# Computing edge features before a scatter instead of after it, and summing them from three bf16 parts, in a graph kernel on one core

## The chip, the cores and the metric

The kernel is one program on one core of a Trainium2 chip. The metric is the device time of one execution in microseconds, as the median of several runs. Engines are called as in the profile: PE (TensorE matmuls), PEld (its weight loads), DVE (VectorE), ACT (ScalarE), POOL (GpSimd), SP (SyncE).

## The reference, cut to what matters

A node table x (6250 x 256) goes through an adapter, a mixture of experts, two graph attention layers and a last mixture with its own attention. Only the adapter's edge part is touched here. 106,250 edges carry 32 numbers each:

```
time_feat = relu(edge_attr @ W_time.T + b_time)        # 106250 x 64
sums      = segment_sum(time_feat, src, num_segments=6250)
counts    = segment_sum(ones, src, num_segments=6250)
node_time_feat = sums / maximum(counts, 1)
```

`edge_attr` is edge_attr_32, the source node of an edge is `src`. The result joins the node features in the adapter's fusion product. Everything is float32.

## The kernel before, in words

`program` runs the stages in order, each a block in which every engine has its own instruction list: `setup`, `sorts` (to about 1413 us of the span), `edge_sums` (to about 2310 us), `norm_T`, `adapter`, normalisation, router and experts, two attention layers, a last attention and the last experts. Each stage ends when all its engines are done.

**sorts** (L218 to L430). Three lists of edges are brought into an order by node block (49 blocks of 128 nodes) and by slots in groups of 512 (256 groups for the list of this case, 4 columns of 128 edges each). DVE does it: it counts each block's edges (L380), PE adds the counts over the partitions (L331, L332), DVE reads these sums (L389) and makes the position of each edge with a match (L356), a scan (L357) and a predicated copy (L365) for each block. Positions of the first 208 of 832 columns (EARLY) are ready first (L401). DVE also makes the low seven bits of each edge's node, `lo0`, and for lists 1 and 2 a payload of 16 bytes for each edge (L420 to L428).

Meanwhile the 832 columns of the first list are moved: SP loads chunks of 16 columns (AC) of edge_attr_32 into a ring of four buffers (L294), ACT adds the low bits as a 33rd number (L322) and POOL scatters one column at a time with an indirect DMA (L274), 128 rows of 33 numbers (132 bytes) to `attr_sorted` in DRAM, which SP has filled with zeros and a node number that matches nothing (L304). A chunk's buffer is free when its scatters have landed (semaphores `done`): ACT and SP wait for that. PE has the sums and the turning of group ends (L335) of three sorts and nothing else.

**edge_sums** (L477 to L616). For each of 256 groups: ACT's queue loads 128 x 4 rows (L531, eight buffers ahead), DVE copies the 32 numbers together (L566), PE transposes them (L593), ACT copies the transpose out of PSUM (L516), PE multiplies it with a block matrix of four W_time (L611), DVE adds the bias (L559), ACT applies ReLU (L527). DVE makes four 128x128 matches of the low bits with 0 to 127 (L569), PE multiplies each with 64 features and a column of ones (L601, four products into pU), and DVE adds the 65 columns into the block's row of `acc` (L553); `grp[0]` says which block a group belongs to. All is float32, for which a product counts as two matmul instructions and two weight loads; a transpose counts as one. The engines run one to four groups apart (`ring`, L621).

At the same time POOL runs `scatter_pool` (L437 to L453): the first 384 columns of list 1, each an indirect DMA of 128 rows of 16 bytes (L449), in two sets of 16 with a wait for the set before. Later stages scatter the rest of lists 1 and 2 in the same way: `norm_T` columns 384 to 440, `adapter` 440 to 588, and so on. The adapter's DVE work has whole-tile additions of 128x1024 (L1357, L1363).

Of the kernel before, what the change touches and what calls it, by code (L numbers as in the profile page):

```python
# [83 lines left out]
class Kernel:  # L84
# [54 lines left out]
    def setup(self, keep):  # L139
# [22 lines left out]
        self.attr_sorted = nc.dram_tensor("attr_sorted", (NG0 * GE, ED + 1), F32).ap()  # L162
# [55 lines left out]
    def sorts(self):  # L218
# [4 lines left out]
        with ctx:  # L223
# [11 lines left out]
            rows = sb("rows", [P, AR, AC, ED + 1])  # L235
            st, dl, var = sb("st", [P, NB, 6]), sb("dl", [P, NB]), sb("var", [P, NB])
            pre = ps("pre", [P, 2, NB])
            zpay = sb("zpay", [P, FILL, PW], I32)
            zattr, zrow = sb("zattr", [P, 8 * (ED + 1)]), sb("zrow", [1, D + 3])
            s_zpay, s_zattr = sem("s_zpay"), sem("s_zattr")  # L240
# [6 lines left out]
            NC = ET // AC  # L247
# [3 lines left out]
            def _(pool):  # L251
                z3 = zattr[:, :].rearrange("p (r c) -> p r c", c=ED + 1)
                pool.memset(z3[:, :, 0:ED], 0.0).then_inc(s_zattr, 1)
                pool.memset(z3[:, :, ED:ED + 1], float(P)).then_inc(s_zattr, 1)
# [9 lines left out]
                for c in range(NC):  # L264
                    j = c % AR
                    pool.wait_ge(ld[j], 16 * (c // AR + 1) + (16 if c == NC - 1 else 0))
# [5 lines left out]
                    for k in range(AC):  # L272
                        t = c * AC + k
                        pool.indirect_dma_start(  # L274
                            out=self.attr_sorted, out_offset=bass.IndirectOffsetOnAxis(ap=pos0[:, t:t + 1], axis=0),
                            in_=rows[:, j, k, :], in_offset=None,
                            bounds_check=last, oob_is_err=False).then_inc(done[j], 16)
# [4 lines left out]
            def _(sp):  # L282
# [6 lines left out]
                def chunk(c):  # L289
                    j = c % AR  # L290
                    if c >= AR:
                        sp.wait_ge(done[j], 16 * AC * (c // AR))
                    n = min(AC, EM - c * AC)
                    sp.dma_start(rows[:, j, 0:n, 0:ED],  # L294
                                 i["edge_attr_32"][0:P * EM, :].rearrange("(p t) a -> p t a", p=P)[:, c * AC:c * AC + n, :])\
                        .then_inc(ld[j], 16)
                    if n < AC:
                        sp.dma_start(rows[0:EL, j, n, 0:ED], i["edge_attr_32"][P * EM:E0, :]).then_inc(ld[j], 16)
# [18 lines left out]
            def _(act):  # L317
                act.wait_ge(s_lo0, 1)
                for c in range(NC):
                    if c >= AR:  # L320
                        act.wait_ge(done[c % AR], 16 * AC * (c // AR))
                    nc.scalar.activation(rows[:, c % AR, :, ED], lo0[:, c * AC:(c + 1) * AC], ACT.Copy).then_inc(s_lo, 1)  # L322
# [4 lines left out]
            def _(pe):  # L327
                for n in range(3):
# [3 lines left out]
                    nc.tensor.matmul(pre[:, 1, :], self.ones[:, :], tot[:, :], start=True, stop=True).then_inc(s_pre, 1)  # L332
                    pe.wait_ge(s_gs, n + 1)
# [3 lines left out]
                    ins.then_inc(s_gt, 1)  # L337

# [138 lines left out]
    def edge_sums(self, acc, scatter=()):  # L477

        nc, i = self.nc, self.i
        ctx, sb, ps, sem = self.scope()  # L480
        A1 = AD + 1
        with ctx:
            rows = sb("rows", [P, DRING, K, ED + 1])
            attr = sb("attr", [P, DRING, K * ED])
            attrT = sb("attrT", [P, 2, P])
            tf = sb("tf", [P, 2, K, A1])
            S = sb("S", [P, DRING, K, P])
            wt = sb("wt", [P, K * AD])
            bt = sb("bt", [P, K, AD])
            pre = sb("pre", [P, 2, K * AD])  # L490
            pT, pF, pU = ([ps(f"{x}{n}", [P, 512]) for n in range(2)] for x in ("pT", "pF", "pU"))
            ld = [sem(f"s_ld{j}") for j in range(DRING)]
            s_w, s_z, s_at, s_T, s_Tc, s_F, s_tf, s_S, s_U, s_acc, s_pre = (sem(x) for x in (
# [1803 lines left out]
```

## Time and profile before

| | us |
|---|---|
| median of 3 runs | 10431.0 (10423.12 to 10436.96) |
| span of the profiled execution | 10342.3 |
| around the span, to the median | 88.7 |
| sorts, in the span | 0 to 1413 |
| edge sums, in the span | 1413 to 2310 |

The profile is one execution. "x" before a number is a count of instructions, busy time is given in us and the mean of one instruction in ns. "remote" stands for a wait that ended by a semaphore whose sender's record had ended before; "issue" is time in which an engine waited for nothing that the profile shows. PEclk is the granted clock of TensorE as a share of full speed: 1.00 is 2.4 GHz, 0.50 is 1.2 GHz.

### The profile page before, as it was taken

To read this page: it belongs to the slowest core of one execution; us is meant where nothing else is said; L and a number is where in the kernel's file an instruction comes from. 1 tells how busy PE (TensorE), PEld (TensorE's weight loads), DVE (VectorE), ACT (ScalarE), POOL (GpSimd) and SP (SyncE) were. 2 spreads that over 40 slices of the span, in tenths; PEclk is the share of its full clock that TensorE was granted. 3 is DMA by queue.
4 is the path that set the end of the run, shared out by engine and by line. 5 is a ranking of instruction groups with operands and counts; after the bars stand their busy time and mean duration, and the time that the engine had idled before them with its cause. 6 is when DMAs were issued, how large, how long until landed. Compare 5 with 4: busy or idle time off the path is not lost. (4 is left out here: it accounts for less than half of the span.)

```text
span 10342.3 us, 116779 instructions
## 1 busy us (share of the span) xinstructions
PE 5494.0 (53%) x22610; PEld 3209.3 (31%) x22610; DVE 5413.1 (52%) x18917; ACT 3566.1 (34%) x11436; POOL 5780.8 (56%) x5781
## 2 busy tenths in 40 slices
PE   0000001593221149936777764777771388888897
PEld 0000000481110025523444432444441134434445
DVE  8577400492200012226666654666663287788777
ACT  0000000241000012214666642666661176666662
POOL 3787767307567740044666654666666566566650
PEclk9999975795565569967878876888885577677658
DMA  4111100010000000002333321333330111111113
GB/s 128 24 21 22 23 11 4 22 40 3 2 23 1 1 1 0 0 12 84 91 91 91 92 64 57 92 91 91 92 89 2 25 23 22 23 23 24 22 22 101
DMA packets 476242, 426.24 MB, mean 41 GB/s; under 512 B 269726, under 2 KB 409876, under 8 KB 475668
## 3 DMA queue, kind: packets, MB, share of 16 engines
q0 software_dynamic: 214016, 282.62, 11.8%
q1 hardware_dynamic: 224020, 120.13, 4.3%
q10 hardware_dynamic: 37632, 17.48, 0.7%
q8 instruction: 159, 2.61, 0.1%
q14 instruction: 415, 3.40, 0.1%
HBM read 341.50 MB, written 78.72 MB: 41 GB/s over the span
## 5 line engine op out<-in xcount | busy, mean ns | idle before, releaser
L449 POOL DMA_INDIRECT pay_sorted<-pay,pos x1856 | 1883.4, 1015 | 1893.7 <-PEq L1217 721.2
L790 POOL DMA_INDIRECT G<-tab_gat,pay x1856 | 1770.4, 954 | 1187.3 <-issue 465.5
L790 POOL DMA_INDIRECT G<-tab_rt,pay x1216 | 1151.5, 947 | 816.0 <-PE pLU L867 353.0
L864 PE MATMUL pU<-G,PM 128*128 128x257 f32 x3712 | 1269.6, 475 | 324.3 <-ACT PM L961 191.4
L274 POOL DMA_INDIRECT attr_sorted<-rows,pos x832 | 972.9, 1169 | 411.3 <-issue 253.4
L864 PEld LDWEIGHTS pU<-G,PM 128*128 128x128 f32 x3712 | 808.2, 241 | 485.4 <-ACT PM L961 235.6
L1679 DVE TENSOR_TENSOR t<-pO,BL 128x1024 f32<-128x1024 f32 (+1 forms) x78 | 90.7, 1163 | 1345.3 <-remote 871.0
L1078 DVE TENSOR_REDUCE mt<-pW 128x4 f32<-128x2048 f32 x304 | 695.4, 2287 | 163.5 <-issue 77.6
L810 PE MATMUL pA<-identb,G 128*20 128x128 bf16 (+1 forms) x3072 | 438.6, 250 | 477.8 <-issue 202.8
L1663 ACT ACTIVATE H<-pH,B 128x512 f32<-128x512 f32 (+1 forms) x312 | 206.6, 663 | 1364.6 <-remote 691.2
L909 ACT ACTIVATE aT<-pA 20x256 bf16<-20x256 bf16 (+1 forms) x1232 | 512.3, 416 | 457.1 <-PE pA L810 170.5
L1626 PE MATMUL pO<-WL,H 128*128 128x256 f32 x1176 | 288.8, 401 | 573.6 <-issue 345.7
L1167 DVE SCALAR_TENSOR_TENSOR e<-e 128x256 f32<-128x256 f32 x928 | 396.2, 427 | 366.8 <-ACT e L955 292.8
L955 ACT ACTIVATE e<-pW,adst 128x256 f32<-128x256 f32 x928 | 438.0, 472 | 298.8 <-DVE mt L1051 209.4
L961 ACT ACTIVATE PM<-pP 128x256 f32<-128x256 f32 x928 | 339.6, 366 | 574.0 <-PE pP L836 380.6
L810 PEld LDWEIGHTS pA<-identb,G 128*20 128x20 bf16 (+1 forms) x3072 | 190.2, 98 | 1081.4 <-issue 1064.6
L836 PE MATMUL pP<-ident,PT 128*128 128x128 f32 x1856 | 490.6, 354 | 0.0
L1051 DVE TENSOR_REDUCE mt<-pW 128x1 f32<-128x256 f32 x928 | 389.6, 420 | 189.5 <-PE pW L820 136.9
L1175 DVE SCALAR_TENSOR_TENSOR acc<-acc,alpha,pU 128x257 f32 x928 | 442.5, 477 | 77.8 <-PE pU L864 41.2
L970 ACT ACTIVATE PT<-e,bias 128x256 f32<-128x256 f32 x928 | 458.3, 494 | 0.7 <-DVE e L1167 0.7
L322 ACT ACTIVATE rows<-lo 128x16 f32<-128x16 f32 x52 | 11.6, 229 | 1291.8 <-DMA attr_sorted<-rows,pos 1223.4
L593 PE MATMUL pT<-ident,attr 128*128 128x128 f32 x256 | 76.0, 297 | 708.5 <-issue 674.4
(324 smaller groups left out, 12213.3 us busy)
## 6 DMA issues: line engine op xcount, KB each, us to landing
pay_sorted<-pay,pos POOLq DMA_INDIRECT x1856
G<-tab_gat,pay POOLq DMA_INDIRECT x1856
G<-tab_rt,pay POOLq DMA_INDIRECT x1216
expert_parts<-pos SPq DMA_DIRECT2D x144, 128.0 KB
yl<-expert_parts SPq DMA_DIRECT2D x36, 512.0 KB, 4.0
attr_sorted<-zattr SPq DMA_DIRECT2D x1, 16896.0 KB, 53.2
rows<-attr_sorted ACTq DMA_DIRECT2D x256, 66.0 KB
attr_sorted<-rows,pos POOLq DMA_INDIRECT x832
```

Source lines behind the costliest of these rows:

```text
L274: pool.indirect_dma_start(out=self.attr_sorted, out_offset=bass.IndirectOffsetOnAxis(ap=pos0[:, t:t + 1], axis=0), in_=rows[:, j, k, :], i ...
L449: pool.indirect_dma_start(out=out, out_offset=bass.IndirectOffsetOnAxis(ap=self.pos[g][:, lo + n:lo + n + 1], axis=0), in_=self.pay[g][:, ...
L790: pool.indirect_dma_start(out=G[:, j, k, 0:R], out_offset=None, in_=table, in_offset=bass.IndirectOffsetOnAxis(ap=pay[:, g % (2 * PART), k ...
L810: ins = nc.tensor.transpose(pA[j % len(pA)][:, k * P:(k + 1) * P], parts[:, k, 0:ROWS], self.identb[:, :])
L836: ins = nc.tensor.transpose(pP[j % 2][:, k * P:(k + 1) * P], PT[:, j % 2, k * P:(k + 1) * P], self.ident[:, :])
L864: ins = nc.tensor.matmul(u[:, 0:F], PM[:, j % 2, k * P:(k + 1) * P], G[:, j, k, 0:F], start=(k == 0), stop=(k == K - 1))
L909: a.activation(aT[:, j % 2, :], pA[j % len(pA)][:, 0:K * P], ACT.Copy).then_inc(s_aT, 1)
L955: a.activation(e[:, j % 2, :], pW[j % 2][:, 0:K * P], ACT.Identity, bias=ad).then_inc(s_y, 1)
L970: a.activation(PT[:, s, :], e[:, s, :], ACT.Exp, bias=bias[:, j % 4:j % 4 + 1]).then_inc(s_PT, 1)
L1078: v.tensor_reduce(mt, pW[:, :, :], AX.X, ALU.max).then_inc(s_max, 1)
L1167: v.scalar_tensor_tensor(e[:, j % 2, :], e[:, j % 2, :], SLOPE, e[:, j % 2, :], ALU.mult, ALU.max).then_inc(s_e, 1)
L1175: v.scalar_tensor_tensor(ac, ac, alpha[:, j, 0:1], pU[j % 2][:, 0:F], ALU.mult, ALU.add).then_inc(s_acc, 1)
```

## The change

The features are now computed in `sorts`, before the scatter. The 832 columns are taken in 208 units of four: PE transposes a unit (128x128), ACT copies the transpose, PE multiplies a row of ones with the bias and then the transpose with the block matrix, ACT writes the ReLU of it into the row buffers. A row has 64 features and the low bits, 65 numbers, 260 bytes, and goes to `feat_sorted`. SP loads chunks into buffers of their own that are free when PE has transposed them; POOL waits for ACT's lo copy alone, which comes behind the chunk's last ReLU. The zero fill is twice as large and is issued behind four chunk loads and eight small loads of weights and biases. PE's sums and turned group ends of the sorts stand at fixed units of its list.

In `edge_sums` a group's 128x4 rows are loaded on SP's queue. ACT casts the features to bf16 (high), DVE subtracts that from them (left), ACT casts the remainder to bf16 (middle), DVE subtracts again and writes bf16 (low). Four matches are made in bf16, four bf16 products add high, middle, low and ones (193 columns) into pU, DVE adds 193 columns into `acc3`, and at the end the three parts are added up into `acc`. The attr copy, the transpose, the features' product, the bias and the ReLU are gone from this stage.

```
@@ setup
-        self.attr_sorted = nc.dram_tensor("attr_sorted", (NG0 * GE, ED + 1), F32).ap()
+        self.feat_sorted = nc.dram_tensor("feat_sorted", (NG0 * GE, AD + 1), F32).ap()
@@ sorts
+            SUMS_AT = (2 * QC - 1, 13 * QC - 1, 30 * QC - 1)
+            NODES_AT = (9 * QC - 1, 25 * QC - 1, 41 * QC - 1)
...
@@ POOL, for each chunk c
-                    pool.wait_ge(ld[j], 16 * (c // AR + 1) + (16 if c == NC - 1 else 0))
                     pool.wait_ge(s_lo, c + 1)
@@ SP
                     if c >= AR:
-                        sp.wait_ge(done[j], 16 * AC * (c // AR))
+                        sp.wait_ge(s_T, (c - AR + 1) * (AC // K))
...
-                sp.wait_ge(s_zattr, 2)
-                sp.dma_start(*self.repeated(self.attr_sorted, zattr[:, :])).then_inc(s_zero, 16)
                 for c in range(AR):
                     chunk(c)
+                sp.wait_ge(s_zw, 1)
+                for k in range(K):
+                    sp.dma_start(wt[k * ED:(k + 1) * ED, k * AD:(k + 1) * AD], i["L0_gnn_W_time"]).then_inc(s_w, 16)
+                    sp.dma_start(bt[:, k * AD:(k + 1) * AD], row(i["L0_gnn_b_time"])).then_inc(s_w, 16)
+                sp.wait_ge(s_zfeat, 2)
+                sp.dma_start(*self.repeated(self.feat_sorted, zfeat[:, :])).then_inc(s_zero, 16)
@@ ACT
+                def copy_attrT(u):
+                    act.wait_ge(s_T, u + 1)
+                    if u >= 2:
+                        act.wait_ge(s_F, u - 1)
+                    nc.scalar.activation(attrT[:, u % 2, :], pT[u % 2][:, 0:P], ACT.Copy).then_inc(s_Tc, 1)
+                def features(u):
+                    c, k = u // QC, u % QC
+                    if k == 0 and c >= AR:
                         act.wait_ge(done[c % AR], 16 * AC * (c // AR))
+                    act.wait_ge(s_F, u + 1)
+                    nc.scalar.activation(rows[:, c % AR, k * K:(k + 1) * K, 0:AD],
+                                         pF[u % 2][:, 0:K * AD].rearrange("p (k c) -> p k c", k=K), ACT.Relu).then_inc(s_tf, 1)
+                copy_attrT(0)
+                for u in range(QC * NC):
+                    if u + 1 < QC * NC:
+                        copy_attrT(u + 1)
+                    features(u)
+                    if u % QC == QC - 1:
+                        c = u // QC
+                        if c == 0:
+                            act.wait_ge(s_lo0, 1)
+                        nc.scalar.activation(rows[:, c % AR, :, AD], lo0[:, c * AC:(c + 1) * AC], ACT.Copy).then_inc(s_lo, 1)
@@ PE
+                def turn(u):
...
+                    if u >= 2:
+                        pe.wait_ge(s_Tc, u - 1)
+                    nc.tensor.transpose(pT[u % 2][:, 0:P], attr[:, c % AR, k * P:(k + 1) * P], self.ident[:, :]).then_inc(s_T, 1)
+                def features(u):
...
+                    if u >= 2:
+                        pe.wait_ge(s_tf, u - 1)
+                    nc.tensor.matmul(pF[u % 2][:, 0:K * AD], self.ones[0:1, :], bt[:, :], start=True, stop=False)
+                    pe.wait_ge(s_Tc, u + 1)
+                    nc.tensor.matmul(pF[u % 2][:, 0:K * AD], attrT[:, u % 2, :], wt[:, :], start=False, stop=True).then_inc(s_F, 1)
+                for u in range(QC * NC):
+                    if u + 1 < QC * NC:
+                        turn(u + 1)
+                    features(u)
+                    if u in SUMS_AT:
+                        list_sums(SUMS_AT.index(u))
+                    if u in NODES_AT:
+                        group_nodes(NODES_AT.index(u))
@@ edge_sums, ACT
+                def high(g, j, turn):
+                    act.wait_ge(ld[j], 16 * (turn + 1))
...
+                    nc.scalar.activation(parts[:, j % 4, :, 0:AD], rows[:, j, :, 0:AD], ACT.Copy).then_inc(s_high, 1)
+                def middle(g, j):
+                    act.wait_ge(s_left, g + 1)
+                    nc.scalar.activation(parts[:, j % 4, :, AD:2 * AD], left[:, j % 2, :, :], ACT.Copy).then_inc(s_mid, 1)
@@ edge_sums, DVE, in the order remainder(g + 1), matches(g), low(g), add(g - 2)
+                    v.tensor_tensor(left[:, j % 2, :, :], rows[:, j, :, 0:AD], parts[:, j % 4, :, 0:AD], ALU.subtract)\
+                        .then_inc(s_left, 1)
...
+                        v.tensor_scalar(S[:, j % 4, k, :], self.iotab[:, :], rows[:, j, k, AD:A1], None, ALU.is_equal)
...
+                    v.tensor_tensor(parts[:, j % 4, :, 2 * AD:3 * AD], left[:, j % 2, :, :],
+                                    parts[:, j % 4, :, AD:2 * AD], ALU.subtract).then_inc(s_low, 1)
...
+                    a = acc3[:, bass.ds(blk, 1), :].rearrange("p a c -> p (a c)")
+                    v.tensor_tensor(a, a, pU[j % 2][:, 0:A3], ALU.add).then_inc(s_acc, 1)
@@ edge_sums, PE
+                    pe.wait_ge(s_low, g + 1)
+                    if g_ge(g, 2):
+                        pe.wait_ge(s_acc, g - 1)
                     for k in range(K):
+                        ins = nc.tensor.matmul(pU[j % 2][:, 0:A3], S[:, j % 4, k, :], parts[:, j % 4, k, :],
                                                start=(k == 0), stop=(k == K - 1))
                     ins.then_inc(s_U, 1)
```

## Rows read from the trace of the kernel before

**Rows 1.** The page, busy time by engine, and POOL in 40 slices.

```profile
PE 5494.0 (53%) x22610; PEld 3209.3 (31%) x22610; DVE 5413.1 (52%) x18917; ACT 3566.1 (34%) x11436; POOL 5780.8 (56%) x5781
...
POOL 3787767307567740044666654666666566566650
```

**Rows 2.** All scatters of the sorts: durations, first and last start.

```profile
L274 POOL DMA_INDIRECT attr_sorted<-rows,pos x832: 969/974/2932, 161.9 to 1387.3; - x167
```

**Rows 3.** Groups of instructions, 0 to 1413 us, the sorts.

```profile
L322 ACT ACTIVATE rows<-lo 128x16 f32<-128x16 f32 x52 | 11.6, 229 | 1291.8 <-DMA attr_sorted<-rows,pos 1223.4 <-DVE lo L386 68.5
...
L356 DVE TENSOR_SCALAR mask<-hi,iota 128x208 bf16<-128x208 bf16 x49 | 13.4, 274 | 9.9 <-DVE posf L365 9.7 <-DVE posf L396 0.2
```

**Rows 4.** Groups of instructions, 1413 to 2310 us, the edge sums.

```profile
L449 POOL DMA_INDIRECT pay_sorted<-pay,pos x384 | 383.7, 999 | 152.5 <-issue 127.1 <-SPq L482 25.4
...
L601 PE MATMUL pU<-tf,S 128*128 128x65 f32 x2048 | 273.5, 279 | 0.4 <-DVE acc L553 0.4
...
L569 DVE TENSOR_SCALAR S<-iota,rows 128x128 f32<-128x128 f32 x1024 | 224.4, 284 | 0.0
...
L559 DVE TENSOR_TENSOR pre<-pF,bt 128x256 f32<-128x256 f32 x256 | 107.2, 419 | 141.2 <-remote 140.3 <-ACT tf L527 0.9
...
L527 ACT ACTIVATE tf<-pre 128x256 f32<-128x256 f32 x256 | 106.8, 417 | 570.6 <-remote 331.3 <-DVE pre L559 113.5 <-issue 103.2
...
L566 DVE COPY attr<-rows 128x128 f32<-128x128 f32 x256 | 57.5, 224 | 19.7 <-issue 10.0 <-DMA rows<-attr_sorted 9.3
...
L553 DVE TENSOR_TENSOR acc<-acc,pU 128x65 f32 x256 | 56.0, 219 | 362.6 <-remote 267.6 <-issue 81.9 <-PE pU L601 12.3
...
L543 DVE MEMSET acc<- 128x3185 f32 x1 | 2.7, 2713 | 0.6 <-issue 0.6
```

**Rows 5.** Stretches: length, PE, PEld, DVE, ACT, POOL, PEclk, DMA share, GB/s.

```profile
318.00:415.00 97.00, 1.30 (x7) 0.50 (x4) 51.25 (x94) 0.92 (x4) 73.83 (x77) 1.00 0.13 24
...
757.00:850.00 93.00, 1.09 (x4) 0.93 (x4) 53.20 (x87) 1.15 (x5) 70.73 (x74) 1.00 0.14 25
...
850.00:1145.00 295.00, 1.86 (x8) 0.84 (x8) 256.19 (x244) 2.53 (x11) 241.34 (x177) 1.00 0.11 20
...
1145.00:1388.00 243.00, 0.00 (x0) 0.00 (x0) 13.29 (x43) 3.37 (x10) 185.06 (x191) 1.00 0.12 23
...
1440.00:1747.00 307.00, 32.97 (x110) 26.35 (x110) 16.52 (x70) 6.94 (x20) 231.47 (x238) 0.50 0.04 4
...
1970.00:2010.00 40.00, 39.17 (x295) 36.36 (x293) 37.94 (x188) 18.54 (x54) 0.00 (x0) 1.00 0.19 46
...
2410.00:2500.00 90.00, 57.42 (x120) 24.46 (x118) 33.86 (x67) 13.11 (x20) 70.30 (x65) 0.65 0.02 2
...
2560.00:2600.00 40.00, 5.72 (x10) 2.78 (x10) 0.51 (x1) 1.96 (x3) 30.55 (x32) 0.51 0.03 2
```

**Rows 6.** Groups of instructions on PE, 1900 to 2310 us.

```profile
L601 PE MATMUL pU<-tf,S 128*128 128x65 f32 x1912 | 244.3, 272 | 0.4 <-DVE acc L553 0.4
```

**Rows 7.** One line, L569, 1970 to 2010 us.

```profile
L569 DVE TENSOR_SCALAR S<-iota,rows x107: 277/280/286, 1969.9 to 2009.9; 128x128 f32<-128x128 f32 x107
```

**Rows 8.** Groups of instructions on DVE in the adapter, 2410 to 2500 us.

```profile
L1357 DVE TENSOR_TENSOR t<-t,bu 128x1024 f32<-128x1024 f32 x6 | 7.3, 1225 | 0.2
...
L1363 DVE TENSOR_TENSOR X<-X,t 128x1024 f32 x4 | 4.9, 1224 | 0.1
...
L1363 DVE TENSOR_TENSOR X<-X,t 128x1024 f32<-128x1024 f32 x2 | 2.4, 1224 | 0.1
```

**Rows 9.** Groups of instructions on POOL, 2410 to 2500 us.

```profile
L449 POOL DMA_INDIRECT pay_sorted<-pay,pos x65 | 70.3, 1081 | 19.8 <-issue 19.8
```

**Rows 10.** One line, L389, DVE reading the sums of each sort.

```profile
L389 DVE TENSOR_SCALAR ni<-pre x3: 209/210/210, 72.9 to 849.1; 128x49 int32<-128x49 f32 x3
```

**Rows 11.** The page, DMA issues: KB, us to landing.

```profile
attr_sorted<-zattr SPq DMA_DIRECT2D x1, 16896.0 KB, 53.2
```

**Rows 12.** Groups of instructions on POOL, 1426 to 1434 us.

```profile
L449 POOL DMA_INDIRECT pay_sorted<-pay,pos x7 | 6.9, 979 | 2.1 <-issue 2.1
```

More of the change, by code:

```diff
@@ L274, in _ @@
                         pool.indirect_dma_start(
-                            out=self.attr_sorted, out_offset=bass.IndirectOffsetOnAxis(ap=pos0[:, t:t + 1], axis=0),
+                            out=self.feat_sorted, out_offset=bass.IndirectOffsetOnAxis(ap=pos0[:, t:t + 1], axis=0),
                             in_=rows[:, j, k, :], in_offset=None,
@@ L327, in _, with list_sums @@
             def _(pe):
-                for n in range(3):
+                def list_sums(n):
                     pe.wait_ge(s_tot, n + 1)
@@ L503, in _ @@
                     self.scatter_pool(pool, s)
[L505 to L528 removed]
+            @block.sync
+            def _(sp):
                 def load(g, j):
[L531 removed]
+                    sp.dma_start(rows[:, j, :, :], rows_v[:, bass.ds(g, 1), :, :].rearrange("p a k c -> p (a k) c"))\
                         .then_inc(ld[j], 16)
@@ L562, in group @@
-                def group(g, j, turn, more):
-                    dve.wait_ge(ld[j], 16 * (turn + 1))
-                    if g_ge(g, DRING):
-                        dve.wait_ge(s_U, g - (DRING - 1))
-                    nc.vector.tensor_copy(attr[:, j, :].rearrange("p (k c) -> p k c", k=K),
-                                          rows[:, j, :, 0:ED]).then_inc(s_at, 1)
-                    for k in range(K):
-                        ins = nc.vector.tensor_scalar(S[:, j, k, :], self.iota[:, :], rows[:, j, k, ED:ED + 1],
-                                                      None, ALU.is_equal)
-                    ins.then_inc(s_S, 1)
-                    if g_ge(g, 2):
-                        before_relu(g - 2, (j - 2) % DRING)
-                    if g_ge(g, 4):
-                        add(g - 4, (j - 4) % DRING)
+                    a = acc3[:, bass.ds(blk, 1), :].rearrange("p a c -> p (a c)")
@@ L577, in _, with group @@
+                    v.tensor_tensor(a, a, pU[j % 2][:, 0:A3], ALU.add).then_inc(s_acc, 1)
+                def group(g, j, turn, more):
+                    if more:
+                        remainder(g + 1, (j + 1) % DRING)
+                    matches(g, j)
+                    low(g, j)
+                    if g_ge(g, 2):
+                        add(g - 2, (j - 2) % DRING)
+                remainder(0, 0)
                 self.ring(dve, NG0, group)
-                before_relu(NG0 - 2, DRING - 2)
@@ L585, in _, with group @@
             @block.tensor
             def _(pe):
-                pe.wait_ge(s_w, 32 * K)
-                def turned(g, j, turn):
-                    pe.wait_ge(s_at, g + 1)
-                    if g_ge(g, 2):
-                        pe.wait_ge(s_Tc, g - 1)
-                    nc.tensor.transpose(pT[j % 2][:, 0:P], attr[:, j, :], self.ident[:, :]).then_inc(s_T, 1)
-                def sums(g, j):
-                    pe.wait_ge(s_tf, g + 1)
-                    pe.wait_ge(s_S, g + 1)
+                def group(g, j, turn, more):
+                    pe.wait_ge(s_low, g + 1)
```

148 lines of the change are left out of this document (67 added, 81 removed).

## The prediction

> **What bounds the kernel now.** I read the page's busy line and POOL's slices first [rows 1]: no engine is over 56% busy, so the limit changes from stage to stage. Next came the scatters of the first stage and the groups of instructions of both stages that the diff touches [rows 2 to 4], then the same stages by stretches [rows 5].
>
> In the **sorts** POOL's 832 scatters set the end: the first begins at 161.9 us, the last at 1387.3; DVE has nearly stopped by 1145 us (13 us of work in the last 243 us). PE does next to nothing there, and ACT's lo copies wait for scatters to land (1223 us) [rows 2, 3, 5].
>
> In the **edge sums** there are two halves. 384 scatters of the first list run from the stage's start, 384 us busy and 127 us of issue, so 511 us; 1912 of the 2048 matmuls into pU, 239 of 256 groups, start after 1900 us [rows 4, 6]. While scatters run, PE is hardly served: 110 matmuls and 110 weight loads in 307 us beside 238 scatters, 0.72 instructions a us, about one for each scatter, at a granted clock of 0.50. Without scatters it did 295 and 293 in 40 us, 14.7 a us, at 1.00 [rows 5]. That pace is not arithmetic: ACT and DVE wait for "remote" 331 us (tf) and 408 us (pre, acc), which is the late report of finished PE work [rows 4]. A group needs 22 PE instructions, hence some 30 us while scatters run. Afterwards DVE sets the pace: 107 matches, 27 groups, in 40 us, 1.48 us a group [rows 7].
>
> One stage shows what relieves PE. The adapter, also under scatters, did 120 and 118 instructions in 90 us, 2.6 a us, and fell to 0.5 later [rows 5]. In those 90 us its twelve additions of 128x1024 with both operands in SBUF (1.22 us each) [rows 8] lengthened the 65 scatters from 974 to 1081 ns [rows 2, 9], 7.0 us or 8% of pause. I therefore price PE's service as 0.72 a us plus 14.7 for each us in which POOL pauses: at 8% that is 1.9, and the adapter had 2.6 with some backlog in it. The chance of one look at SBUF falling into an addition is 16% (14.7 us of 90), its mean rest 0.61 us: 0.10 us for a scatter, as measured (0.107). So a short operation costs POOL by the square of its length.
>
> **Part 1, features in the sorts.** A unit of 4 columns is 10 PE instructions (transpose 2, bias product 4, main product 4, f32 products counting twice), two ACT copies and four hand-overs; 208 units, 2.5 PE instructions for each scatter, where clean service gives 0.92.
> - Start: the sums of sort 0 come after unit 7, and ACT stands at the lo copy until 72.9 us, about when DVE now reads the sums [rows 10]. Four more units, each some four durations of 0.42 us (transpose, copy, product, ReLU, after tf [rows 4]), put positions and POOL off by **+7 us** (0 to 10).
> - Clean stretches (318 to 415, 757 to 850, 1145 to 1388 us) hold 77+74+191 = 342 scatters with a period of 1.27 us [rows 5]. POOL must pause s in each until 0.72(1.27+s) + 14.7s = 2.5, so s = 0.10 us: **+35 us**. If PE enters each stretch with three chunks ready, 144 scatters are free of it and 20 us remain; 100 us if each hand-over is late as well.
> - In the other stretches scans already lengthen the scatters: 177 in 295 us is 1.67 us each, 0.40 us of pause, service 7 for a need of 2.5: nothing. DVE's waits for sums 2 and 3 have 240 us of cover behind DVE's end; without it they would add what POOL's positions come late, here nothing, since POOL needs sort 0 alone.
> - The zero fill doubles: 16896 KB landed in 53.2 us [rows 11], so 33280 KB in 105 us, issued behind four chunk loads and eight small loads of weights. POOL's first scatter is at 162 us: nothing, and up to +40 us if the fill shares the queues with the loads of keys. SP's chunk loads now wait for the transposes, not for landed scatters, so they come earlier; behind the fill on SP stand key loads of sorts 1 and 2 and X, needed hundreds of us later. Rows of 260 bytes instead of 132 leave POOL's issue alone: 0.974 us is what it takes for rows of either list [rows 2, 12]. I take zero (bounds -5 and +20).
>
> **Part 2, edge sums.** DVE keeps seven operations: out go the attr copy (224) and pre (419), two remainders of 128x256 (0.42 each, as pre) come in, four matches become bf16 (0.25 for 128 wide, from 0.274 for 208 [rows 3]; before 0.284), the addition grows from 65 to 193 columns (0.35, between 0.219 and 0.419). Before, 0.224+4x0.284+0.419+0.219 = 2.00 us of durations passed in 1.48 us [rows 4, 7]; now 0.84+1.00+0.35 = 2.19, so **1.62 us** a group (1.45 to 1.85). ACT's two casts (0.42 each) and PE's 8 instructions fit beside it. SP's loads double to 130 KB, DMA share 0.19 before: hidden.
> - Under the scatters a group needs 8 PE instructions, 5.0 a us at DVE's pace. Two remainders in 1.62 us meet half of the scatters for 0.21 us on average: 0.11 us in 1.28, p = 8.5% at full pace, less in proportion below it. Then the share of full pace is 0.72/(5.0-14.7x0.085) = 0.19, 8.5 us a group. The 5 to 7 groups of the unhindered start come on top.
> - Sum: 519 us of scatters hold 61+7 groups; 188 left at 1.62 us are 305 us; resuming and tail 35 us, as now (511+237x1.48+35 = 897); the last additions and the copy over 49x64 columns 7 us, from the clearing of 128x3185 in 2.7 us [rows 4]. Together 866: **-31 us**. Without any pause of POOL a group takes 11.1 us: 53 groups, -14 us, and +33 with 1.85 us a group; with 1.45 us and p = 12% -85 us.
> - Clearing the wider sums is 8 us instead of 2.7, beside scatters: nothing; if PE had been free of starvation, +5.
>
> Sum: 7+35-31 = **+11 us**. The profiled execution is 10342.3 us and 88.7 us around it, together just the median of 10431.0; so 10442 us.
>
> **A rule that speaks against the first price.** In a clean stretch with matches running, 7 scatters took 979 ns each, like undisturbed ones [rows 12], so matches of f32 cost POOL nothing that shows. The Trainium skill, "SBUF — State Buffer", section "SBUF: two separate sides", says that DVE operations with two SBUF inputs, or in a two-port mode, lock a port pair that POOL's descriptor writing needs, for the whole instruction. By that the bf16 matches too would hold POOL up; the next paragraph prices it.
>
> **Rivals.**
> - *POOL is held up enough to set PE free* (faster). If additions and matches, 1.8 of 2.19 us, each stop POOL, its pause passes (5.0-0.72)/14.7 = 29% at full pace and starvation never sets in: all 256 groups run inside the scatters, which stretch to 511x1.3 = 660 us, and the stage ends some 20 us later: -215, in all -173, **10258 us**. For it: the adapter held out for 90 us at 8%. Against: the matches of before [rows 12].
> - *Edge groups stay tied to hand-overs, not to PE counts* (slower). If a group takes 25 us under scatters whatever it contains (four hand-overs through ACT, DVE and PE), 27 groups are done and 229x1.62 = 371 us follow: 511+371+42 = 924, +27; in all +69, **10500 us**. For it: "remote" waits stand on ACT and DVE, not on PE [rows 4].
> - *The features become the bound of the sorts* (slower). POOL has (1387.3-161.9)/208 = 5.9 us for a unit. If four hand-overs need 7 us, 208x7 = 1456 us: +231 in place of 35, **10640 us**; it decides from 5.9 us on. Against: POOL's own stops set PE free.
>
> **Chances.** Forecast 0.46 (own range 10390 to 10490), first rival 0.22, second 0.18, third 0.14. About 0.2% (21 us) is what a measurement can tell. Of the forecast 0.14 lies under 10410, 0.19 within 21 us and 0.13 above. Faster 0.22+0.14 = 0.36; same 0.19; slower 0.18+0.14+0.13 = 0.45. The range 10245 to 10560 takes in most of the first rival and the second; outside remain the third's greater part and the first's far end.
>
> **What would show it.** Right: L274's successor idles some 30 us for ACT's lo copy, all after 318 us; 60 to 75 groups are added up before the 384th scatter; afterwards 24 to 25 groups in 40 us; the stage of the edge sums lasts 850 to 880 us. Wrong: scatters of the edge stage longer than 1.1 us on average with PE clock 1.00 beside them (first rival), under 35 groups by the end of the scatters (second), or an ACT wait before each chunk of scatters (third). A first scatter after 175 us would show the fill or the late sums mispriced.

## The result, and the profile after

The changed kernel takes 10500.2 us in the median of 20 runs, the kernel before 10447.6 us in 20 runs on the same chips. The ratio, over fast runs alone, is 1.0034, 95% interval 1.0019 to 1.0048, so 20 to 50 us slower; the plain medians lie 53 us apart. Slower was the largest of the three chances, and the forecast was +11 us. The profiled execution of the changed kernel spans 10458.6 us.

The two stages that the diff touches, and the rest, from the first instruction of each stage in the trace:

| | before | before, profiled again (e4) | after |
|---|---|---|---|
| edge sums begin at | 1413.0 | 1412.4 | 1461.1 |
| length of the edge sums, us | 898 | 896 | 870 |
| everything behind them, us | 8031 | 8041 | 8128 |

So the sorts lose 48 us and the edge sums give back 28: +20 us in the touched stages, where the sum of the prediction had +42 and -31. The rest belongs to stages that nobody edited. It differs from one execution to the next: 8041, 8112, 8056 and 8020 us in e4, e1, e2 and e3 (more on this at e4).

**The sorts.** The row of the scatters with what POOL waited for (us, times), in the profile after; [rows 2] answers to its first line:

```profile
L282 POOL DMA_INDIRECT feat_sorted<-rows,pos x832: 966/972/2907, 169.5 to 1447.4; - x167
its engine sat idle before it (us, times) until:
  issue: 251.0, 824
  DVE pos L461: 165.0, 1
  ACT rows L353: 53.3, 7
```

The first scatter is 7.6 us later (161.9 before), the last 60 us later (1387.3 before). Between the two lie 53.3 us in seven waits for ACT's lo copy, which stands behind the features of its chunk. The next two lines say why the start is late, and that the fill is not the reason: DVE reads the sums of sort 0 at 80.4 us (72.9 in [rows 10]), and the fill, twice as large as in [rows 11], lands long before 160 us.

```profile
L449 DVE TENSOR_SCALAR ni<-pre x3: 209/209/210, 80.4 to 889.3; 128x49 int32<-128x49 f32 x3
...
feat_sorted<-zfeat SPq DMA_DIRECT2D x1, 33280.0 KB, 92.3
```

**The edge sums.** Groups of instructions of this stage, 1461 to 2331 us, after; they answer to [rows 4]:

```profile
L509 POOL DMA_INDIRECT pay_sorted<-pay,pos x384 | 392.2, 1021 | 135.9 <-issue 122.5 <-POOLq L127 13.3
L656 PE MATMUL pU<-parts,S 128*128 128x193 bf16 x1024 | 206.7, 357 | 700.6 <-DVE acc L629 368.2 <-issue 326.5 <-DVE parts L620 5.8
L616 DVE TENSOR_SCALAR S<-iotab,rows 128x128 bf16<-128x128 bf16 x1024 | 191.7, 256 | 7.0 <-issue 7.0
...
L609 DVE TENSOR_TENSOR left<-rows,parts 128x256 f32<-128x256 f32 x256 | 107.7, 421 | 129.6 <-issue 124.1 <-remote 3.1 <-PE pU L656 2.2
...
L629 DVE TENSOR_TENSOR acc<-acc,pU 128x193 f32 x256 | 89.7, 350 | 293.7 <-issue 293.0 <-PE pU L656 0.5 <-DVE acc L629 0.2
```

PE has half of the matmuls into pU that it had (1024 for 2048) and waits for DVE; a remainder costs 0.42 us, the wide addition 0.35, a match 0.256 where the f32 match had 0.284. Stretches of the same profile (columns as in [rows 5]):

```profile
1145.00:1388.00 243.00, 87.91 (x172) 41.97 (x171) 35.75 (x67) 20.64 (x76) 172.33 (x166) 1.00 0.10 29
...
1510.00:1740.00 230.00, 14.55 (x72) 7.88 (x72) 33.82 (x132) 15.37 (x39) 174.49 (x179) 1.00 0.07 13
...
2040.00:2080.00 40.00, 20.27 (x101) 10.95 (x100) 40.00 (x177) 21.07 (x50) 0.00 (x0) 1.00 0.32 84
```

In the second line, beside 179 scatters, PE gets 144 instructions in 230 us, 0.63 a us, about what [rows 5] has (0.72). This stretch is called starved below, and the one without scatters free. The granted clock is 1.00 here where it was 0.50 before, so a low clock is not the cause. In the third, without scatters, DVE is busy for all 40 us. The additions and scatters of the starved stretch (1510 to 1740 us), and the matches of the free one (2040 to 2080 us):

```profile
L629 DVE TENSOR_TENSOR acc<-acc,pU 128x193 f32 x18 | 6.4, 356 | 128.6 <-issue 128.6
```
```profile
L509 POOL DMA_INDIRECT pay_sorted<-pay,pos x179 | 175.2, 979 | 55.5 <-issue 55.5
```
```profile
L616 DVE TENSOR_SCALAR S<-iotab,rows x101: 242/247/254, 2039.9 to 2079.7; 128x128 bf16<-128x128 bf16 x101
```

Eighteen groups in 230 us are 12.8 us each; 101 matches in 40 us are 1.59 us a group (1.48 in [rows 7]). By the end of the scatters 51 groups are added up, before it was 16. So the change makes a group 2.4 times cheaper while scatters run (12.8 us for 30.8) and 7% dearer afterwards, and 205 of 256 groups run afterwards.

What holds a group up in this starved stretch is not PE, though the count of its instructions looks like that of before. Four lines from the timeline, at the end of the scatters:

```profile
1974.92 1.51 POOL L509 DMA_INDIRECT pay_sorted<-pay,pos  x1 [0.30 <-issue]
...
1981.19 0.80 PE L656 MATMUL pU<-parts,S 128*128 128x193 bf16 x4 [11.12 <-DVE acc L629]
...
1991.30 0.35 DVE L629 TENSOR_TENSOR acc<-acc,pU 128x193 f32 x1 [7.09 <-issue]
...
1991.80 0.81 PE L656 MATMUL pU<-parts,S 128*128 128x193 bf16 x4 [9.81 <-DVE acc L629]
```

PE runs the four matmuls of a group in one go, in 0.8 us, and its semaphore is updated at 1982.01 us, right at their end. Then PE stands until DVE's next addition. In between DVE works through instructions of its list that compute nothing on tiles: registers, waits and branches, written DVEq. Those that read a group's block number (L624), first in the starved stretch (1510 to 1740 us), then in the free one (2040 to 2080 us):

```profile
L624 DVEq FUSED_REGOPS  x38: 5/701/728, 1513.3 to 1739.5; - x38
L624 DVEq TENSOR_LOAD <-grp x19: 689/698/727, 1514.7 to 1738.1; - x19
L624 DVEq SEQ_ASSERT  x18: 6/700/729, 1517.5 to 1727.6; - x18
```
```profile
L624 DVEq FUSED_REGOPS  x50: 53/124/190, 2041.0 to 2079.7; - x50
L624 DVEq TENSOR_LOAD <-grp x25: 300/304/316, 2041.1 to 2079.3; - x25
L624 DVEq SEQ_ASSERT  x25: 23/23/27, 2041.6 to 2079.9; - x25
```

The middle one of each kind takes 0.70 us beside scatters, and 0.02 to 0.30 us without them. Over all recorded DVEq instructions the mean is 0.71 us against 0.09 us. In the kernel before, and in e3 below, they stay at 0.09 us beside scatters, and there it is PE's report that comes late: a group's addition starts 53.7 us (before) and 42.5 us (e3) after the recorded end of its matmuls, where it is 0.2 and 0.1 us without scatters. So two different lists are slow, and 0.63 and 0.72 need not have one cause. Nor does it stop with the last scatter, which ends at 1976.4 us: the next two groups still take 10.6 and 10.5 us. Why a list slows down beside scatters is not shown.

### The profile page after: what moved, and what is told of

It reads as the page before. It is cut to its first block and busy times, and to the rows that moved or that the text cites. A ratio compares the mean times of both kernels' runs of the same rounds, so it can differ in the third digit from the quotient of the medians.

```text
span 10458.6 us, 115297 instructions
## 1 busy us (share of the span) xinstructions
PE 5884.2 (56%) x21858; PEld 3219.3 (31%) x21858; DVE 5469.3 (52%) x18919; ACT 3708.3 (35%) x11852; POOL 5784.0 (55%) x5782
## 5 line engine op out<-in xcount | busy, mean ns | idle before, releaser
L282 POOL DMA_INDIRECT feat_sorted<-rows,pos x832 | 974.7, 1171 | 469.2 <-issue 251.0
L385 PE MATMUL pF<-bt,ones 1*128 1x256 f32 x416 | 253.1, 710 | 649.7 <-ACT rows L341 433.1
L656 PE MATMUL pU<-parts,S 128*128 128x193 bf16 x1024 | 206.7, 357 | 700.6 <-DVE acc L629 368.2
## 6 DMA issues: line engine op xcount, KB each, us to landing
feat_sorted<-zfeat SPq DMA_DIRECT2D x1, 33280.0 KB, 92.3
```

Of the source, the lines that this page charges most:

```text
L282: pool.indirect_dma_start(out=self.feat_sorted, out_offset=bass.IndirectOffsetOnAxis(ap=pos0[:, t:t + 1], axis=0), in_=rows[:, j, k, :], i ...
```

## The experiments

All times are against the kernel before on the same chip. Theory 1 is the prediction's: PE is served at 0.72 instructions a us beside scatters issued back to back and at 14.7 in POOL's pauses. The expectations count PE's instructions by it; in versions of the changed kernel that count is no more than the pace of the groups, eight instructions each.

**e1, paced scatters.** In `scatter_pool`, called with a pace from the edge sums of the changed kernel:

```
+                if pace is not None:
+                    pace(n, hi - lo)
                 pool.indirect_dma_start(
...
+                def pace(n, total):
+                    need = n * NG0 // total - 6
+                    if need > 0:
+                        pool.wait_ge(s_low, need)
```

> The changed kernel, but in the edge sums POOL issues scatter n only when DVE is done with group n*2/3 - 6 (a wait on a constant), so that scatters and groups end together. Theory 1 (PE gets about 0.7 instructions a us while scatters are issued back to back and 14.7 for each us in which POOL pauses, so a small pause in each scatter pays): 0.72T + 14.7(T-490) = 2048 gives a stage of about 600 + 20 us where the changed kernel has 868, so the whole is about 245 us faster than the changed kernel, some 210 below before. Rival (short pauses do not help, PE recovers only after POOL has stopped for long): the stage stays at 868 us or gets longer, since POOL now waits for slow groups as well.

Measured: the stage takes 593 us, the whole 10154 us, ratio 0.977 (0.972 to 0.982). Two stretches of its edge sums, and the scatters of the second:

```profile
1500.00:1760.00 260.00, 87.60 (x436) 47.43 (x434) 181.24 (x764) 89.38 (x218) 179.79 (x171) 0.50 0.24 57
1800.00:1960.00 160.00, 79.77 (x396) 43.33 (x394) 157.50 (x692) 82.91 (x198) 127.86 (x101) 0.50 0.33 82
```
```profile
L511 POOL DMA_INDIRECT pay_sorted<-pay,pos x101 | 129.3, 1281 | 32.4 <-issue 32.4
```

Short pauses are enough. In the first stretch a scatter comes every 1.52 us and PE gets 3.3 instructions a us, five times as much as unpaced. The second stretch was expected by nobody: POOL is behind its schedule and waits for nothing, yet each scatter lasts 1.281 us instead of 0.97, one comes in each 1.59 us, which is DVE's time for a group, and PE keeps DVE's pace (790 instructions in 160 us, 4.9 a us, which is all a group asks for). The scatters have fallen into step with DVE's list: nearly all of them begin within 0.1 us of DVE's second subtraction, and are held up by it. That is a state like the first rival's, and the groups keep their full pace while it lasts.

**e2, no bias product.** Four of a unit's ten PE instructions are left out (and with them the bias):

```
-                    nc.tensor.matmul(pF[u % 2][:, 0:K * AD], self.ones[0:1, :], bt[:, :], start=True, stop=False)
                     pe.wait_ge(s_Tc, u + 1)
-                    nc.tensor.matmul(pF[u % 2][:, 0:K * AD], attrT[:, u % 2, :], wt[:, :], start=False, stop=True).then_inc(s_F, 1)
+                    nc.tensor.matmul(pF[u % 2][:, 0:K * AD], attrT[:, u % 2, :], wt[:, :], start=True, stop=True).then_inc(s_F, 1)
```

> The changed kernel without the bias product in the sorts (the bias is left out, four of a unit's ten PE instructions). Theory 1 (PE instructions are counted): need 1.5 instead of 2.5 for each scatter, so POOL's waits for the lo copies fall from 53 us to 0 to 15 us and the last scatter of the sorts begins 40 to 50 us earlier, at about 1400 us. Rival (a unit costs its hand-overs between PE and ACT, which stay as they are): 45 to 55 us of waits and a last scatter at 1440 to 1450 us.

The scatters of its sorts:

```profile
L282 POOL DMA_INDIRECT feat_sorted<-rows,pos x832: 967/974/2911, 166.4 to 1424.4; - x167
...
  ACT rows L353: 27.8, 3
```

Three waits of 28 us in all instead of seven of 53, and a last scatter 23 us earlier; the whole is at 0.998 (0.995 to 1.002) of before. The waits follow the count of PE instructions, but less steeply than theory 1 says: it had 0 to 15 us, the rival 45 to 55.

**e3, sums in f32.** The sorts of the change with f32 matches and products on the scattered features (ACT copies them beside ones, DVE makes four f32 matches and adds 65 columns):

```
+                    nc.scalar.activation(tf[:, j % 4, :, 0:AD], rows[:, j, :, 0:AD], ACT.Copy).then_inc(s_tf, 1)
...
-                        v.tensor_scalar(S[:, j % 4, k, :], self.iotab[:, :], rows[:, j, k, AD:A1], None, ALU.is_equal)
+                        ins = v.tensor_scalar(S[:, j % 4, k, :], self.iota[:, :], rows[:, j, k, AD:A1], None, ALU.is_equal)
...
-                        ins = nc.tensor.matmul(pU[j % 2][:, 0:A3], S[:, j % 4, k, :], parts[:, j % 4, k, :],
+                        ins = nc.tensor.matmul(pU[j % 2][:, 0:A1], S[:, j % 4, k, :], tf[:, j % 4, k, :],
                                                start=(k == 0), stop=(k == K - 1))
```

> The changed sorts, but edge sums in float32 as before: ACT copies the features beside a column of ones, DVE makes four f32 matches and adds 65 columns, PE multiplies in f32 (16 PE instructions a group where the three bf16 parts have 8; DVE has 5 operations in place of 7). Theory 1: under the scatters 16/0.7 = 23 us a group, some 25 groups by their end; afterwards about 1.0 to 1.2 us a group where the changed kernel has 1.6: 500 + 231 x 1.1 + 35 = 790 us for the stage against 868, 70 to 80 us faster than the changed kernel. Rival (f32 products at 16 instructions set the pace afterwards too): 1.5 us a group and a stage of 880 us.

A miss: the stage takes 929 us, the whole is at 1.0076 (1.0039 to 1.0112). Its starved and its free stretch:

```profile
1500.00:1940.00 440.00, 36.96 (x152) 33.84 (x152) 21.28 (x95) 7.92 (x19) 333.42 (x332) 0.50 0.05 7
2030.00:2380.00 350.00, 350.00 (x1642) 350.00 (x1642) 217.34 (x1027) 85.37 (x205) 0.00 (x0) 0.50 0.30 77
```

0.69 PE instructions a us beside scatters, as theory 1 has it. But in the free stretch PE is busy throughout, 1642 pairs of weight load and matmul in 350 us, 0.213 us each, eight pairs a group: 1.71 us, at a granted clock of 0.50. In the kernel before, at 1.00, 295 pairs took 40 us, 0.136 us each over a mix of three kinds of products [rows 5]. So f32 sums make PE the bound of this stage behind the scatters, and the bf16 parts, with PE busy half of the time, take it off PE. That the clock makes the pairs longer is not shown: executions of e3 with a mean granted clock of 0.79 take 10400 to 10467 us, those with 0.71 take 10413 to 10502 us.

**e4, the kernel before, profiled again.**

> The kernel before, profiled once more: how far stages that no diff touches differ between two executions of one program. In the two profiles so far everything after the edge sums takes 8031 us before and 8128 us after. If the 97 us belong to the change (other addresses, other states left behind), this run shows 8031 again within 15 us; if they are chance from execution to execution, it lies nearer to 8080 to 8130.

8041 us behind the edge sums, like the first time, which alone would speak for a cost of the change there. But e2 and e3, whose later stages are the changed kernel's, have 8056 and 8020 us. (e1 has 8112, but 64 us of it lie in the adapter, which takes 321 us there, as in e5, and 257 before.) In the profile after, 40 of the 97 us lie in the first two attentions (1439 us each against 1418 and 1420), and e1 to e3 have 1416 to 1420 in both. So it is more likely chance of the execution than the change; with one profile of each this is not shown.

The run settles another thing, the clock. The same program, in the stretch of [rows 5] that was granted 0.50:

```profile
1440.00:1747.00 307.00, 32.97 (x110) 26.36 (x110) 16.30 (x70) 6.94 (x20) 232.03 (x238) 1.00 0.04 4
```

The same 220 PE instructions beside 238 scatters at 1.00, so the granted clock does not set this pace.

**e5, the kernel before, paced.** As e1, with the wait on the semaphore of DVE's matches:

```
+                        pool.wait_ge(s_S, need)
```

> The kernel before (f32 sums, features in the edge sums, 22 PE instructions a group) with the pacing of e1: POOL issues scatter n only when DVE has made the matches of group n*2/3 - 6. Theory 1 (service 0.72 a us plus 14.7 for each us of pause, so the count of PE instructions decides): 0.72T + 14.7(T-490) = 5632 gives T = 833 and a stage of 850 us against 896, some 45 us faster than before. Rival (a threshold: once scatters come slower than every 1.5 us or so, PE is served at full pace whatever it has to do): 384 x 1.5 + 20 = about 600 us for the stage, some 290 us faster than before, and the changed kernel's smaller count of PE instructions is worth nothing once the scatters are paced.

```profile
1500.00:2000.00 500.00, 413.59 (x2124) 370.27 (x2124) 291.55 (x1358) 134.55 (x388) 281.51 (x289) 0.72 0.12 27
```

A stage of 677 us, between the two; the whole at 0.983 (0.976 to 0.990). PE gets 8.5 instructions a us with a scatter every 1.73 us. Theory 1 with 0.72 and 14.7 has the right direction and is too low here: 0.45 us of pause in 1.73 gives 4.5 by it.

**e6 and e7, a fixed pause.** The changed kernel; after each scatter of the edge sums POOL clears a tile, of 128x16 in e6 and 128x256 in e7, and waits for no group:

```
+            if idle is not None and n:
+                pool.wait_ge(idle[1], n - 1)
+                pool.memset(idle[0], 0.0).then_inc(idle[1], 1)
             pool.indirect_dma_start(
```

> The changed kernel; in the edge sums POOL clears a tile of 128x16 (about 0.115 us) after each scatter and waits for nothing of the groups. Scatters then start about every 1.40 us instead of 1.28. Theory 1: pause 8%, service 1.9 a us, 4.2 us a group instead of 11.6; 538 us of scatters hold 128 groups, 128 x 1.6 + 40 us follow: a stage of about 780 us. Rival (threshold): either still starved, 11 us a group, 49 groups, 538 + 207 x 1.6 + 40 = 910 us, or all groups at 1.6 us and a stage of 560 us.

> As e6 with a tile of 128x256 (about 0.31 us), scatters about every 1.6 us. Theory 1: pause 20%, service 3.6 a us, 2.2 us a group: 256 groups are done after 565 us, inside 384 x 1.6 = 615 us of scatters; a stage of about 635 us. Threshold: 1.6 us a group, all groups done after 415 us, the same stage of 635 us; the two differ in the pace of the groups. Third possibility (the hand-shake of e1 and not the pause is what helped): 10 us a group or more and a stage over 900 us.

e6 takes 694 us for the stage, which no theory had (780, 910 or 560), e7 608 for 635 expected. Three stretches of e6, and POOL and the additions in the second and third:

```profile
1500.00:1600.00 100.00, 14.53 (x72) 7.89 (x72) 30.48 (x120) 12.75 (x35) 76.10 (x140) 1.00 0.12 26
1640.00:1810.00 170.00, 85.72 (x425) 46.47 (x424) 169.65 (x746) 89.83 (x213) 153.56 (x213) 1.00 0.33 85
1850.00:2000.00 150.00, 22.61 (x112) 12.28 (x112) 49.14 (x196) 21.71 (x56) 118.18 (x212) 1.00 0.12 27
```
```profile
L512 POOL DMA_INDIRECT pay_sorted<-pay,pos x107 | 136.6, 1276 | 16.5 <-issue 8.6 <-POOL idle L511 0.2
...
L633 DVE TENSOR_TENSOR acc<-acc,pU 128x193 f32 x107 | 37.3, 349 | 0.3 <-issue 0.3
...
L512 POOL DMA_INDIRECT pay_sorted<-pay,pos x106 | 105.6, 996 | 21.2 <-issue 20.4 <-POOL idle L511 0.2
...
L633 DVE TENSOR_TENSOR acc<-acc,pU 128x193 f32 x28 | 9.9, 354 | 65.9 <-issue 65.1 <-PE pU L660 0.8
```

One kernel shows both states. In its first and last stretch a pause of 0.12 us lets 1.4 to 1.5 PE instructions a us through (theory 1: 1.9) and a group takes 5.4 to 5.9 us; DVE's list is slow again, 0.32 us on average for its register instructions in the last stretch; in the middle one the scatters are in step with DVE, 1276 ns each, and 107 groups pass in 170 us, 1.59 us each. It falls into step and out of it by itself.

In e7 a pause of 0.36 us brings a scatter every 1.60 us, and groups at DVE's full pace throughout (220 in 350 us):

```profile
1500.00:1850.00 350.00, 176.94 (x878) 96.10 (x879) 349.77 (x1535) 184.67 (x438) 310.63 (x437) 1.00 0.33 85
```
```profile
L512 POOL DMA_INDIRECT pay_sorted<-pay,pos x219 | 234.0, 1069 | 39.5 <-issue 37.2 <-POOL idle L511 2.4
L511 POOL MEMSET idle<- 128x256 f32 x218 | 79.3, 364 | 0.0
```

So the pause does it, not the hand-shake of e1.

**e8, no scatters in the edge sums.**

```
-            k.edge_sums(acc0, scatter=[(1, 0, 384)])
+            k.edge_sums(acc0)
```

> The changed kernel with the 384 scatters of the edge sums left out (those columns of list 1 are not brought into order). All theories: 256 x 1.6 + 20 to 30 us = 430 to 440 us for the stage, which says what the scatters cost it: 868 - 435 = 433 us. If PE were slow for a reason other than the scatters, the first 500 us would still hold only some 50 groups.

```profile
L629 DVE TENSOR_TENSOR acc<-acc,pU x256: 341/349/358, 1477.1 to 1881.8; 128x193 f32 x128
```

256 additions in 405 us from the first group on, a stage of 428 us. The 384 scatters cost it 442 us in the changed kernel, most of the 515 us that they take: beside them little is done.

**e9 to e12, versions.** e9 is e7 with the sums of sort 0 behind unit 3; e10 the kernel before with the same pause; e11 and e12 have the pause in all scatters up to the experts' stage, e11 on the changed kernel with the early sums, e12 on the kernel before. The edit of `SUMS_AT` is in e9 and e11, the pause in all four.

```
-            SUMS_AT = (2 * QC - 1, 13 * QC - 1, 30 * QC - 1)
+            SUMS_AT = (QC - 1, 13 * QC - 1, 30 * QC - 1)
...
+            if self.idle is not None and n:
+                pool.wait_ge(self.s_idle, self.n_idle)
+                pool.memset(self.idle[:, :], 0.0).then_inc(self.s_idle, 1)
+                self.n_idle += 1
```

> The changed kernel with the pause of e7 (a clearing of 128x256 after each scatter of the edge sums) and with the sums of sort 0 behind unit 3 instead of unit 7, ahead of the lo copy that ACT stands at. If the late sums are what put POOL's start off by 7.6 us, the first scatter starts at 162 to 163 us (169.5 in the changed kernel) and the sorts end 7 us earlier; if the cause is the fill or PE's load, it stays at 169. With a stage of 608 us for the edge sums and 41 us more than before in the sorts: 896 - 608 - 41 = 247 us faster than before, a ratio of 0.976.

> The kernel before with the same pause in its edge sums. Its groups need 22 PE instructions, 15 a us at full pace. With e5 (8.5 served a us at a pause of 0.45 us in 1.72) and e7 (at least 5.0 at 0.33 in 1.60): 5 to 7 a us, 3.1 to 4.4 us a group, 140 to 195 groups in 614 us of scatters, a stage of 740 to 830 us. If the threshold idea were right with its edge under 1.6 us, all groups would be done inside the scatters: 635 us. So the change would be worth 130 to 220 us in this stage once the scatters pause, where it is worth 28 without.

> As e9, with the pause in all scatters up to the experts' stage. If the starvation found in the edge sums is the same in the experts (654 scatters, one body of 64 PE instructions in about 82 us beside them and about 10 us after them), the pause lets bodies through at 11 to 13 us while the scatters stretch to 654 x 1.6 = 1046 us: the experts' stage shrinks from 1568 to 1070 to 1150 us, the whole to about 9600 to 9700 us. If the experts are slow for another reason, their stage grows by the pauses, 654 x 0.33 = 215 us, to 1780.

> The kernel before with the pause in all scatters up to the experts' stage. The stages after the edge sums as in e11; the difference from e11 is that of e10 from e9, 90 to 180 us slower than e11 (the change's gain in the edge sums under paused scatters less its 41 us in the sorts).

| | us | ratio to before | edge sums begin | edge sums, us | experts, us |
|---|---|---|---|---|---|
| e9 | 10142.1 | 0.975 (0.970 to 0.980) | 1454 | 608 | 1568 |
| e10 | 10153.0 | 0.976 (0.972 to 0.980) | 1412 | 711 | 1568 |
| e11 | 9502.9 | 0.914 (0.911 to 0.917) | 1451 | 609 | 980 |
| e12 | 9566.9 | 0.920 (0.917 to 0.923) | 1406 | 713 | 980 |

e9 came as expected. The others came out below their ranges: the edge sums of e10 711 us for 740 to 830, the experts of e11 980 us for 1070 to 1150, and e12 64 us behind e11 for 90 to 180. One unedited stage gives some of the gain back: the adapter takes 288 to 321 us in the versions that pause in the edge sums alone (e1, e5 to e7, e9, e10), 228 to 270 in those without a pause, and 250 in e11 and e12, which pause there too. Why was not tried.

The first scatter of e9:

```profile
L284 POOL DMA_INDIRECT feat_sorted<-rows,pos x832: 966/972/2922, 162.0 to 1440.5; - x167
...
  ACT rows L355: 55.3, 7
```

At 162.0 us: the 7.6 us were the late sums alone, and the 55 us of waits stay. In e10 PE gets 6.5 instructions a us (2927 in 450 us) and a group takes 3.4 us:

```profile
1500.00:1950.00 450.00, 394.64 (x1464) 331.99 (x1463) 217.27 (x932) 92.46 (x267) 396.72 (x608) 0.53 0.11 22
```

The experts, in the profile after and in e11, 800 us of each, with the scatters running:

```profile
2950.00:3750.00 800.00, 142.29 (x304) 75.42 (x302) 26.16 (x45) 24.74 (x36) 609.28 (x588) 0.58 0.02 1
```
```profile
2650.00:3450.00 800.00, 758.47 (x2418) 451.49 (x2416) 214.11 (x372) 205.87 (x311) 705.32 (x1078) 0.98 0.02 1
```

606 PE instructions beside 588 scatters, one for one, against 4834 beside 1078 entries of POOL (a scatter and a clearing each counted). DVE's register instructions take 0.05 us on average in both. The starvation is no matter of the edge sums; a clearing of 0.33 us after each scatter takes 588 us from the experts. In e11 their last 150 us are scatters alone, so a smaller pause there may give more; that was not tried. e11 is the fastest version, 8.6% under the kernel before.

## Why the prediction was right

**The start, +7 us**, measured 7.6, and e9 shows the cause that was named. The fill took 92.3 us for 105 estimated and stayed hidden; DVE's waits for later sums (44 us) stayed hidden too, since DVE ends ahead of POOL.

**The clean stretches, +35 us**, measured 53.3 in seven waits. They stand where the prediction put them, in or right behind the three stretches. Its size was off: it let POOL pause 0.10 us at each scatter, evenly, and PE be served at 14.7 a us in these pauses. In fact POOL runs through its ready chunks unhindered and then stands for a whole chunk's features, 7.6 us on average and up to 13.7. That their products wait for copies between PE and ACT is argued from the list, not shown. e2 cuts what a scatter needs from PE above the 0.92 of clean service from 1.6 to 0.6 instructions, and the waits from 53 to 28 us.

**The end of the sorts** was left as it was; it is 12 us shorter. From the last scatter to the first of the edge sums 14 us pass after and 26 us before (1387.3 to 1413.6). So the stage loses 48 us and not 60. It belongs to the change: all profiles with the new sorts have 14 us there, those with the old ones 24 to 30. Why was not tried.

**A group at DVE's pace, 1.62 us**, measured 1.59, and 1.58 without any scatter (e8). That DVE alone set the old pace of 1.48 us is not settled: PE was busy for 39.2 of those 40 us and DVE for 37.9 [rows 5]. The lower bound of -85 us takes 5.0 PE instructions a us; at 1.45 us a group it is 5.5, and the bound about -70 us.

**A group beside the scatters, 8.5 us**, is the step that failed, in its size and in its cause. The prediction had PE served at 0.72 instructions a us plus what the pause from remainders, p = 8.5%, lets through. Measured are 12.8 us, and 51 groups done, not 68. The pause hardly came: a scatter of the starved stretch takes 979 ns for 972 undisturbed, 7 ns where the forecast's 8.5 us a group stand for about 20 (an estimate: 0.11 us x 1.62/8.5). And what the next group waits for is DVE's own list, at 0.7 us an instruction, and not PE. That the bound for no pause, 11.1 us and 53 groups, lies near is luck.

In the other state nearly every scatter meets a subtraction, and the pause is 0.31 us in 1.59, 19%. Which operations hold a scatter up can be counted in the first stretch of e1, by what DVE runs 0.13 us after the scatter's start: the second subtraction 1245 ns on average (27 scatters), the first 1109 (36), a bf16 match 976 (25), the addition out of pU 972 (9), nothing 972 (51). So it is the two subtractions, whose operands both lie in SBUF, and not "additions and matches". The Trainium skill, "SBUF — State Buffer", section "SBUF: two separate sides", has a DVE operation in a two-port mode, or one with two SBUF inputs (this one only against a POOL operation that reads SBUF), hold for the whole instruction the port pair that POOL's descriptor writing needs. The trace agrees for the subtractions, 0.3 us a scatter in step; for the bf16 matches it shows 4 ns.

The stage came out at 870 us for 866 by errors that cancel: 515 us of scatters for 519, 205 groups of 1.59 us (326 us) for 188 of 1.62 (305 us), and 29 us for 42 of resuming, the last additions and the end.

**The rivals.** The third (the features as the bound of the sorts, +231 us) fell: POOL waited 53 us. The second (25 us a group whatever it contains) fell: 12.8 us in the changed kernel, 22.4 from addition to addition in e3, 30.8 before. In the last two it is 1.40 us for each of 16 and 22 PE instructions, so there the count decides; in the changed kernel it is DVE's list. The first is real as a state, in e1 and e6, through the subtractions alone, but the changed kernel leaves it within 30 us of the stage's start and does not return.

**The sum** of the touched stages is +20 us for +11: +48 for +42 in the sorts, -28 for -31 in the edge sums, each with errors of both signs inside, so the nearness is in part luck. The 88.7 us that the prediction puts around the span of the profile before are not that: in the runs on record the time lies 1.8 us above the span (10460.4 and 10458.6 us in the profile after), so that profile is of an execution some 87 us faster than the median. Whether the other 15 us up to the ratio's middle are chance of the other stages can't be told from single profiles, which differ by 100 us there.

## What to carry to other kernels

Where one engine issues small indirect DMAs back to back and others crawl beside it, count what they get through beside the DMAs; if it is as little as here (51 of 256 groups in 515 us), a short idle instruction after each DMA can be worth more than moving work: here 0.33 us a scatter bought 8%, and the rewrite of two stages cost 0.3%. Look also at which engine's list is slow, registers and waits included, before pricing a count: PE's count fitted the kernel before and not the changed one. Judge a rewrite under both conditions: the same change loses 0.3% without pauses and gains 0.7% with them (e11 against e12; 7 of the 64 us are the early sums), as its lighter groups only pay where the lists run at pace. And a stage that waits for an engine's list is not free because that engine was idle on average: PE did nothing in the sorts, and its work still came too late there for 53 us.

## What the runs showed of the hardware that was not expected

- PE instructions run in a us, by the time from scatter to scatter, with the granted clock: 0.63 to 0.72 at 1.28 to 1.33 us (0.50 and 1.00), 1.4 to 1.5 at 1.41 to 1.43 (e6, 1.00), 6.5 at 1.48 (e10, 0.53), 3.3 at 1.52 (e1, 0.50), 8.5 at 1.73 (e5, 0.72). It grows much faster than the pause. It is not one curve: the kernels have different lists, and in e1 and e6 DVE's register instructions are slow as well (0.14 and 0.32 us on average).
- Register and wait instructions on DVE took 0.71 us on average beside back-to-back scatters in the changed kernel, 0.09 us without scatters, and 0.09 us beside scatters in the kernel before.
- Two states of one program: scatters of 0.98 us and starved groups, or scatters of 1.28 us in step with DVE and groups at full pace; e6 changes between them twice.
- The granted clock was 1.00 in some starved stretches (after, e4) and 0.50 in others (before, e3), with the same pace, 0.6 to 0.7 a us. The bf16 matmuls of the edge sums took the same time at 0.50 (e1, 79.77 us for 396) as at 1.00 (after, 20.27 us for 101).
- Everything behind the edge sums took 8020 to 8128 us in five profiles of kernels that do the same there (before, after, e2 to e4).
